# A two-layer token model on one core: mix and preparation in one block, the experts' first layer one group ahead, the last batch's routed rows scaled by VectorE

## The chip, the cores and the metric

One NeuronCore of one Trainium2 chip runs the whole program in one launch. The metric is device time in microseconds (us), lower is better. Engine names: TensorE (PE), its weight loads (PEld), VectorE (DVE), ScalarE (ACT), GpSimd (POOL), SyncE (SP). A line such as L1267 is a line of the kernel before.

## The reference, cut to what matters

The input is token numbers, 8 batches of 512; the model width D is 192. Six stages follow, each adding to a running stream `h`:

```python
h = tok_ref(x, ...)                                  # gathered rows, a trace of outer products
h = h + attn_ref(layernorm(h), ...)                  # linear attention
h = h + ffn_ref(layernorm(h), ...)                   # soft mixture of 64 experts
h = h + attn_q_ref(layernorm(h), ...)                # attention, 8-bit fake quantisation
x = h' + attention(layer_norm(h'), ...)              # h' = layernorm(h)
h = h + x + moe(layer_norm(x), top 2 of 8 experts)   # routed experts
```

In the soft mixture each of 64 experts gets one slot per batch: `h1 = gelu(xs @ w1 + b1)` (192 to 768), `ys = h1 @ w2 + b2` (768 to 192), and the rows are mixed back by `y = combine @ ys`. The quantised attention starts with `fake_quant(x) @ fake_quant(w_qkv)`: the scale of `x` is the largest absolute value of the normalised rows over all batches, divided by 127, and each weight matrix has such a scale of its own. In the last stage every row goes to the two experts with the largest logits.

## The kernel before, in words

`kernel_program` runs six stage functions one after the other. Each consists of blocks (`nc.Block`): in a block each engine has its own list of instructions with semaphores between them, and all engines meet at its end. After a stage, `recycle` adds a small block in which GpSimd clears semaphores.

**The experts' block of `soft_moe`** (L1205 to L1290). The 64 experts are taken in 16 groups of four (`GE` = 4, `NGR` = 16). The weights of one group are in one of three slots (`RING` = 3); a slot is filled in two parts by `ring_load` (L934): part 0 is the first layer with its bias (per expert 576 KB), part 1 the second layer (576 KB per expert), and both parts of a slot count on one semaphore. Groups 0 to 2 are sent in the block before. In this block SyncE sends part 0 of group g once the first layer of group g-3 is done, then part 1 once the second layer of g-3 is done (L1273 to L1277). TensorE's order for each group is:

- the first layer (L1245, L1248, L1253), after waiting for both parts of the slot (L1242)
- after ScalarE's gelu (L1228), six transposes (L1259)
- after VectorE's copy out of PSUM (L1217), the second layer in 48 small matmuls (L1267)

ScalarE then copies the result (L1232) and GpSimd stores it in DRAM (L1286). After the last group GpSimd loads everything back (L1289), and the block ends.

**The mix block** (L1295 to L1331). VectorE adds the second bias (L1299). For each batch TensorE multiplies four times (L1329), VectorE adds the product to the stream `m.H` (L1304) and takes statistics (L1308, four `bn_stats`), and ScalarE stages the next combine weights (L1317). The matmul buffers alternate between two batches.

**The preparation block of `quantised_attention`** (L1372 to L1431). VectorE turns all the statistics into means and variances in six linked steps (`ln_constants`, L151 to L156); ScalarE takes the square root (L430), VectorE the reciprocal (L425). Then VectorE normalises each batch (L1406, four instructions) and takes its absolute maximum (L1409), and takes the maxima of the two weight matrices (L1416, L1417); GpSimd reduces over the partitions (L1399); VectorE makes scales (L1369 to L1421), scales the weights (L1422, L1426) and rounds them to bf16 (L1423, L1425, L1427). GpSimd fills buffers with zeros and constants at the start of the block (L1391 to L1397). ScalarE begins the next block with L1447.

**The routed attention's last block** (L2369 to L2707). After the loop over batches, VectorE finishes the last batch: norm (L2564), stream sum (L2569), the two best experts (L2577 to L2585), the places of its rows (L2591 to L2602). GpSimd multiplies the normalised rows by the layer norm's gain and adds its offset (L2672, L2675), sends them by indirect transfers to DRAM, once for each of the two experts (`send`, L2687), and copies the last batch's rows (L2703) for the second of them. SyncE sends the weights of tiles 0 and 1 once the tile tables are made, waits for all sent rows, loads the rows of tiles 0 and 1 (`load_rows`, L2717, L2718), and sends the weights of tiles 2 and 3 (`load_weights`, L2724), and then the block ends.

**The routed experts' block** (L2743 on): 39 tiles of 256 rows. TensorE turns rows (L2781), computes first layers (L2791, L2795) one tile ahead and second layers (L2806). SyncE's loop is `next_rows(n)`, which waits until the rows of tile n-2 are copied, and from tile 4 on also `load_weights(n)`.

## Time and profile before

| | |
|---|---|
| time, median of 3 runs | 2439.43 us (2437.96 to 2439.54) |
| the profiled execution | 2437.44 us, of which the span is 2435.4 us |
| busy in it | PE 1882.9 us, DVE 1502.0, ACT 1057.0, POOL 398.8 |
| mean granted TensorE clock | 0.832 of full speed |
| experts' block (first layer to the last second layer) | 598.5 to 774.6 us |
| mix block, from VectorE's first work | 783.6 to 809.1 us |
| preparation block, to ScalarE's first work in the next | 809.1 to 839.7 us |
| last batch of the routed attention to the first routed tile | 2008.2 to 2057.6 us |
| routed tiles | 2057.6 to 2400.4 us |

How to read it: all times are from the span's start. The busy share of the page is a mean over stages with different limits, so each of the stretches is read by itself. A granted clock of 1.00 is 2.4 GHz and 0.50 is 1.2 GHz. In the timeline a line gives start, duration, engine, line and operation, and in brackets how long the engine was idle and what ended that. A row of busy time by stretch gives the stretch and its length, the busy time of PE, PEld, DVE, ACT and POOL (x instructions), the granted clock, the mean busy share of the 16 DMA engines (it can come out a little over 1) and GB/s.

### The profile page before, as it was taken

What the parts mean: (1) busy time and instruction counts of PE and PEld (TensorE: products, weight loads), DVE (VectorE), ACT (ScalarE), POOL (GpSimd) and SP (SyncE); (2) the same over time, 40 slices, a digit from 0 to 9 for tenths busy, and PEclk for the clock granted to TensorE, in tenths of its full rate; (3) what the DMA queues carried; (4) which work ended last, traced back from release to release, by engine and by line L of the source; (5) the groups of instructions that cost most, each with busy time, mean ns of one, the idle gap of its engine ahead of it and who ended that gap; (6) DMA issues with size and microseconds to landing.
All of it is one profiled execution on the core that took longest, in us unless ns stands there. A gap on an engine that the chain in (4) does not pass through costs nothing. (4 is left out here: it accounts for less than half of the span.)

```text
span 2435.4 us, 31261 instructions
## 1 busy us (share of the span) xinstructions
PE 1882.9 (77%) x9780; PEld 1010.5 (41%) x9804; DVE 1502.0 (62%) x2512; ACT 1057.0 (43%) x1856; POOL 398.8 (16%) x597
## 2 busy tenths in 40 slices
PE   3868789858886353777678857999899983999994
PEld 2735655535333320000112225443133333888883
DVE  4558459955101687999878874999788893111114
ACT  1100322213101267999889954333476660222221
POOL 5000000000221010222100003331023343222221
PEclk8989999969886575555589968997699995999997
DMA  3011110024994003333001007767777613566664
GB/s 84 1 38 33 52 33 18 20 90 165 403 410 194 13 1 125 126 125 125 26 19 39 26 15 113 121 118 118 85 86 98 99 30 129 177 203 204 203 206 182
DMA packets 147791, 264.96 MB, mean 109 GB/s; under 512 B 28865, under 2 KB 115986, under 8 KB 142679
## 3 DMA queue, kind: packets, MB, share of 16 engines
q1 hardware_dynamic: 135750, 242.10, 37.4%
q0 software_dynamic: 10768, 18.19, 2.3%
q10 hardware_dynamic: 1152, 3.15, 0.3%
q8 instruction: 67, 1.10, 0.2%
q14 instruction: 54, 0.43, 0.1%
HBM read 221.85 MB, written 57.71 MB: 115 GB/s over the span
## 5 line engine op out<-in xcount | busy, mean ns | idle before, releaser
L1677 PE MATMUL ps<-arena 128*128 x376 | 194.8, 621 | 108.0 <-ACT ps L1719 60.2
L1719 ACT ACTIVATE ps<-ps,arena 128x512 f32<-128x512 f32 x384 | 256.6, 1121 | 6.3 <-POOL arena L1703 6.3
L1687 DVE TENSOR_REDUCE arena<-ps 128x1024 f32 x192 | 232.8, 1224 | 24.1 <-PE ps L1677 9.9
L1719 ACT ACTIVATION_READ_ACCUMULATOR ps<-ps,arena 128x1 f32 x384 | 234.7, 668 | 0.0
L2151 DVE TENSOR_REDUCE arena<-ps 128x1024 f32 x192 | 221.0, 1216 | 10.7 <-PE ps L2314 8.4
L2520 ACT ACTIVATE arena<-ps 128x1024 f32<-128x1024 f32 x192 | 185.0, 1020 | 97.4 <-PE ps L2402 95.8
L2850 DVE TENSOR_TENSOR arena<-ps,arena 128x384 f32<-128x384 f32 x39 | 21.7, 557 | 286.9 <-PE ps L2806 286.9
L2830 ACT ACTIVATE arena<-ps,arena 128x256 f32<-128x256 f32 x234 | 89.5, 481 | 235.9 <-PE ps L2795 230.0
L2314 PE MATMUL ps<-arena 96*128 96x512 bf16 x500 | 163.8, 433 | 23.9 <-DVE arena L2151 11.1
L1884 ACT ACTIVATE arena<-ps 128x1024 f32<-128x1024 f32 x192 | 178.7, 1048 | 8.0 <-DVE arena L1904 4.6
L528 PE MATMUL ps<-arena 96*128 96x456 f32 (+1 forms) x512 | 169.9, 482 | 8.8 <-DMA arena<-la_xt 5.2
L2806 PE MATMUL ps<-arena 128*128 128x192 f32 x936 | 162.5, 330 | 0.7 <-DVE arena L2850 0.7
L2806 PEld LDWEIGHTS ps<-arena 128*128 128x128 f32 x936 | 151.0, 190 | 13.6 <-issue 13.6
L1904 DVE TENSOR_SCALAR arena<-arena 128x1024 bf16<-128x1024 f32 x192 | 128.5, 690 | 29.1 <-ACT arena L1884 14.9
L1677 PEld LDWEIGHTS ps<-arena 128*128 128x128 bf16 x384 | 25.6, 110 | 276.4 <-ACT ps L1719 197.5
L1837 PE MATMUL ps<-arena 128*128 (+1 forms) x368 | 113.6, 389 | 15.8 <-DMA arena<-arena 13.5
L528 PEld LDWEIGHTS ps<-arena 96*128 96x128 f32 x512 | 96.0, 196 | 71.4 <-issue 55.0
L2765 POOL DMA_INDIRECT routed_out<-arena x78 | 74.7, 958 | 283.2 <-DVE arena L2850 271.3
L1217 DVE COPY arena<-ps 128x768 f32<-128x768 f32 x16 | 15.3, 957 | 155.3 <-PE ps L1259 155.3
L2791 PE MATMUL ps<-arena 128*128 128x256 f32 x468 | 109.8, 385 | 0.9 <-DVE arena L2844 0.9
L2468 PE MATMUL ps<-arena 128*32 128x512 f32 x768 | 106.3, 626 | 4.0 <-ACT arena L2520 2.2
L2402 PE MATMUL ps<-arena 99*128 99x512 bf16 x384 | 104.8, 397 | 2.4 <-ACTq L137 2.4
(384 smaller groups left out, 3258.2 us busy)
## 6 DMA issues: line engine op xcount, KB each, us to landing
arena<-in_sm_w_dram SPq DMA_DIRECT2D x128, 576.0 KB
arena<-in_re_w_dram SPq DMA_DIRECT2D x39, 1252.0 KB, 5.8
arena<-ra_parts SPq DMA_DIRECT2D x192, 192.0 KB, 9.1
routed_in<-routed_in SPq DMA_DIRECT2D x8, 3332.0 KB, 14.2
ra_parts<-arena SPq DMA_DIRECT2D x48, 192.0 KB, 2.5
arena<-routed_in SPq DMA_DIRECT2D x39, 196.0 KB, 5.4
arena<-la_xt SPq DMA_DIRECT2D x16, 384.0 KB, 3.4
arena<-arena SPq DMA_DIRECT2D x64, 96.0 KB, 2.2
```

What stands on the lines that cost most here:

```text
L528: ins = pe.matmul(ps[:, 2 * (t % 2) + bank, to:to + w], XTs[j][:, c, t * P:(t + 1) * P], Wx[:, kind, c, at:at + w], start=(c == 0), stop=( ...
L1677: ins = pe.matmul(ps[:, 2 * (n % 4) + t % 2, :], QM[j][:, h, t * P:(t + 1) * P], KI[:, b, h // HG, :], start=True, stop=True)
L1687: v.tensor_reduce(MXq[:, b, 2 * u:2 * u + 2, at_head(h)], ps[:, 2 * (n % 4):2 * (n % 4) + 2, :], AX.X, ALU.max).then_inc(s_lk, 1)
L1719: ins = act.activation(bank, bank, ACT.Exp, bias=nb[n % 4][:, t % 2:t % 2 + 1], scale=c_reg, accum_out=RS[:, b, t, at_head(h):at_head(h) + 1])
L1837: ins = pe.matmul(ps[:, 2 * (n % 3) + q, :], QM[j][:, h, c * P:(c + 1) * P], QI[:, bass.ds(b, 1), g, :].rearrange("p o s -> p (o s)"), sta ...
L1884: act.activation(PF[n % 3], ps[:, 2 * (n % 3):2 * (n % 3) + 2, :].rearrange("p a s -> p (a s)"), ACT.Exp, scale=c_reg).then_inc(pe_.sem, 1)
L1904: v.tensor_scalar(PB[n % 3], PF[n % 3], MAGIC, MAGIC, ALU.add, ALU.subtract).then_inc(rd.sem, 1)
L2151: v.tensor_reduce(MX[:, bass.ds(b, 1), 2 * (n % 2):2 * (n % 2) + 2, n // 2].rearrange("p o t -> p (o t)"), ps[:, 2 * (n % 2):2 * (n % 2) + ...
L2314: ins = pe.matmul(ps[:, t, :], ST_[j][0][0:KR, h, t * P:(t + 1) * P], ST_[j][1][0:KR, h, :], start=True, stop=True)
L2520: act.activation(PF[e // 2 % 2][:, 2 * (e % 2):2 * (e % 2) + 2, :], ps[:, 2 * (e % 3):2 * (e % 3) + 2, :], ACT.Exp, scale=HD ** -0.5).then ...
L2791: pe.matmul(unit(k), wr[:, k * P:(k + 1) * P], XT[j][:, 0, :], start=True, stop=False)
L2806: ins = pe.matmul(ps[:, 7, h * D:(h + 1) * D], HT[j][:, k, h * P:(h + 1) * P], wr[:, at:at + D], start=(k == 0), stop=(k == KH - 1))
```

## The change

It has four parts.

1. In the experts' block part 0 of a slot gets a semaphore of its own. TensorE does the first layer of group g+1 before the transposes and the second layer of group g; only the second layer waits for part 1. VectorE and ScalarE follow that order, and SyncE sends part 0 of group g+1 ahead of part 1 of group g.
2. The mix block is removed, and its work is in the preparation block. The bias sum and the staged combine weights go to new buffers. Batches go in four pairs: mix, statistics, and the constants of that pair; ScalarE normalises (a scale and a bias for each row); VectorE takes the maxima of the pair before. The weights' maxima, scales and rounding stand between the pairs, and their scaling is ScalarE's. GpSimd reduces twice, first for the weights, then for the rows.
3. For the last batch VectorE multiplies and adds gain and offset, right after the stream sum, and ScalarE makes the copy.
4. The weights of tiles 2 and 3 are sent at the start of the routed experts' block.

The diff's core:

```diff
+    done = (m.ring_first, m.ring)[part][r]
     for q in range(GE):
-        sp.dma_start(m.EW[:, GE * r + q, w], io.sm_w[GE * g + q][:, w]).then_inc(m.ring[r], 16)
+        sp.dma_start(m.EW[:, GE * r + q, w], io.sm_w[GE * g + q][:, w]).then_inc(done, 16)
...
+            hidden(0)
+            for g in range(NGR):
+                if g + 1 < NGR:
+                    hidden(g + 1)
+                out(g)
...
             for g in range(RING, NGR):
-                hp.wait(sp, g - RING, 1)
-                ring_load(sp, m, io, B1, g, 0)
+                if g == RING:
+                    hp.wait(sp, g - RING, 1)
+                    ring_load(sp, m, io, B1, g, 0)
+                if g + 1 < NGR:
+                    hp.wait(sp, g + 1 - RING, 1)
+                    ring_load(sp, m, io, B1, g + 1, 0)
                 yp.wait(sp, g - RING, 1)
                 ring_load(sp, m, io, B1, g, 1)
...
+        @block.vector
+            v.tensor_tensor(YE, YB, b2[:, None, :].to_broadcast([NE, B, D]), ALU.add).then_inc(s_b, 1)
...
+            between = None, weight_maxima, weight_scales, round_weights
+            for k in range(NP):
+                mix(2 * k)
+                l(mix(2 * k + 1))
+                ln_constants(v, l, m.ST[:, two, :, :]..., mean, flat(m.var[:, two, :]))
+                v.sem_inc(s_var, 1)
+                if k:
+                    for b in (2 * k - 2, 2 * k - 1):
+                        row_max(b)
+                    between[k]()
+                v.wait_ge(s_std, k + 1)
+                l(v.reciprocal(rstd, work))
+                v.scalar_tensor_tensor(out=flat(m.wk[2][:, two, :]), in0=mean, scalar=-1.0, in1=rstd, ...
+            for b in (B - 2, B - 1):
+                row_max(b)
...
+        @block.scalar
+            for b in range(B):
+                act.activation(CS[:, b, :], CT[:, b, :], ACT.Copy).then_inc(cst.sem, 1)
...
+            for k in range(NP):
+                act.activation(m.wk[1][:, two, :], m.var[:, two, :], ACT.Sqrt, ...)
+                act.wait_ge(s_k, k + 1)
+                for b in (2 * k, 2 * k + 1):
+                    for t in range(T):
+                        ins = act.activation(m.X[:, b, t, :], m.H[:, b, t, :], ACT.Identity,
+                                             bias=m.wk[2][:, b, t:t + 1], scale=m.rstd[:, b, t:t + 1])
+                if k == 2:
+                    act.activation(Wf, Wf, ACT.Identity, bias=magic[0:DC], scale=inv[0:DC, 1:2])
+                    act.activation(WPf, WPf, ACT.Identity, bias=magic, scale=inv[:, 2:3])
...
-            load_weights(sp, io, m, 2)
-            load_weights(sp, io, m, 3)
...
+            def scale_last():
+                gt.wait(v, p, 2)
+                v.tensor_tensor(rows, rows, lg_[:, None, :].to_broadcast([P, T, D]), ALU.mult).then_inc(s_gb, 1)
+                v.wait_ge(s_gb, 2 * p + 1)
+                v.tensor_tensor(rows, rows, lb_[:, None, :].to_broadcast([P, T, D]), ALU.add).then_inc(s_gb, 1)
...
-                scale(p + 1)
+                if p + 1 < B - 1:
+                    scale(p + 1)
...
-            pool.tensor_copy(XA[B % 2][:, :, HEAD:RW], XA[1 - B % 2][:, :, HEAD:RW]).then_inc(s_gb, 1)
+            act.activation(XA[B % 2][:, :, HEAD:RW], XA[1 - B % 2][:, :, HEAD:RW], ACT.Copy).then_inc(s_gb, 1)
...
             for n in range(2, NW):
+                load_weights(sp, io, m, n)
+            for n in range(2, NW):
                 next_rows(n)
```

## Rows read from the trace of the kernel before

**Rows 1.** Busy time by stretch: the experts' block, and its loads' time.

```profile
598.50:774.60 176.10, 140.90 (x1440) 63.26 (x1440) 16.83 (x31) 19.04 (x32) 30.93 (x60) 0.84 0.89 353
605.50:757.50 152.00, 122.02 (x1266) 55.91 (x1265) 14.82 (x28) 15.96 (x28) 28.89 (x56) 0.85 1.02 405
```

**Rows 2.** Timeline of TensorE over the last two groups.

```profile
758.60 2.16 PE L1267 MATMUL ps<-arena 128*32 128x192 f32 x48 [1.05 <-DVE arena L1217]
761.81 0.88 PE L1245 MATMUL ps<-arena 4*128 4x384 f32 x2 [1.05 <-issue]
...
767.92 1.57 PE L1259 MATMUL ps<-arena 128*128 128x128 f32 x6 [0.97 <-ACT arena L1228]
...
770.54 4.07 PE L1267 MATMUL ps<-arena 128*32 128x192 f32 x48 [1.05 <-DVE arena L1217]
```

**Rows 3.** Busy time by stretch: two stretches in which the clock is low.

```profile
598.50:604.50 6.00, 5.66 (x36) 1.17 (x36) 0.00 (x0) 1.23 (x2) 0.00 (x0) 0.72 0.01 3
727.00:741.00 14.00, 11.98 (x90) 4.78 (x90) 1.06 (x2) 1.12 (x2) 0.63 (x2) 0.51 1.02 411
```

**Rows 4.** Timeline of the mix block, VectorE.

```profile
783.62 1.75 DVE L1299 TENSOR_TENSOR arena<-arena 64x1536 f32<-64x1536 f32 x1 [13.13 <-PEq L1205]
...
788.89 0.96 DVE L1304 TENSOR_TENSOR arena<-ps,arena 128x768 f32 x1 [3.52 <-PE ps L1329]
...
791.47 0.96 DVE L1304 TENSOR_TENSOR arena<-ps,arena 128x768 f32 x1 [0.30 <-PE ps L1329]
```

**Rows 5.** Groups by line: normalising, maxima, and a small ScalarE copy.

```profile
L1406 DVE TENSOR_SCALAR arena<-arena x32 | 10.0, 374 | 0.5 <-DVE arena L425 0.5
L1409 DVE TENSOR_REDUCE arena<-arena x8 | 7.6, 952 | 1.3 <-DVE arena L1406 1.3
...
L1232 ACT ACTIVATE arena<-ps 128x192 f32<-128x192 f32 x16 | 5.3, 330 | 87.9 <-PE ps L1267 87.9
```

**Rows 6.** Timeline of the preparation block.

```profile
811.22 0.88 DVE L156 TENSOR_SCALAR arena<-arena 128x32 f32<-128x32 f32 x1
...
812.18 1.28 ACT L430 ACT_TABLE_LOAD   x1 [9.88 <-DVE arena L156]
...
833.19 1.34 DVE L1416 TENSOR_REDUCE arena<-arena 96x1 f32<-96x1152 f32 x1
...
838.51 0.46 DVE L1427 TENSOR_SCALAR arena<-arena 128x576 bf16<-128x576 f32 x1
839.73 1.03 ACT L1447 ACTIVATE arena<-arena 128x768 f32<-128x768 f32 x1 [25.93 <-DVEq L137]
```

**Rows 7.** Timeline of the routed attention's last batch.

```profile
2018.38 0.17 DVE L2557 TENSOR_SCALAR arena<-arena 128x4 f32<-128x4 f32 x1
...
2021.84 1.89 POOL L2687 DMA_INDIRECT routed_in<-arena  x1 [0.64 <-POOL arena L2680]
...
2028.43 0.19 DVE L2571 TENSOR_SCALAR arena<-ps 128x32 f32<-128x32 f32 x1 [5.61 <-PE ps L2429]
...
2029.44 1.80 POOL L2675 TENSOR_TENSOR arena<-arena 128x768 f32<-128x768 f32 x1
2029.74 1.52 DVE L2582 CAST arena<-arena 128x8 f32<-128x8 uint32 x1
...
2031.56 0.69 DVE L2585 TENSOR_TENSOR arena<-arena 128x32 bf16<-128x32 f32 x1
...
2034.71 1.03 POOL L2687 DMA_INDIRECT routed_in<-arena  x1 [2.42 <-DVE arena L2602]
```

**Rows 8.** Timeline from the last rows' load to the routed tiles.

```profile
2053.13 0.57 SPq L2718 DMA_DIRECT2D arena<-routed_in  x1
2054.46 1.48 SPq L2724 DMA_DIRECT2D arena<-in_re_w_dram  x2
2057.60 1.09 PE L2781 MATMUL ps<-arena 128*128 128x128 f32 x4 [24.93 <-DVEq L137]
...
2066.93 0.66 PE L2781 MATMUL ps<-arena 128*128 128x128 f32 x4
```

More of the change, by code:

```diff
@@ L1223, in _, with gelu @@
             yc.start(act)
-            for g in range(NGR):
+            def gelu(g):
                 j = g % 2
@@ L1290, in _ @@
             pool.wait_ge(s_ty, 16)
[L1292 to L1331 removed]
+    m.mix = CT, YB, b2
 def quantised_attention(nc, m, io):
@@ L1401, in _, with mix @@
         @block.vector
         def _(v):
-            ln_v(v)
-            with v.Fori(0, B) as b:
+            hh.start(v)
+            l = Link(v, s_ch)
+            flat = lambda a: a.rearrange("p b t -> p (b t)")
+            v.tensor_tensor(YE, YB, b2[:, None, :].to_broadcast([NE, B, D]), ALU.add).then_inc(s_b, 1)
+            def mix(b):
+                yo.wait(v, b, 1)
+                v.tensor_tensor(m.H[:, b, :, :], ps[:, b % 2 * T:b % 2 * T + T, 0:D], m.H[:, b, :, :],
+                                ALU.add).then_inc(hh.sem, 1)
+                hh.wait(v, b, 1)
@@ new lines, in _ @@
+            for k in range(NP):
+                mix(2 * k)
+                l(mix(2 * k + 1))
+                two = slice(2 * k, 2 * k + 2)
+                mean, rstd, work = (flat(a[:, two, :]) for a in (m.mean, m.rstd, m.wk[1]))
+                ln_constants(v, l, m.ST[:, two, :, :].rearrange("p b t s -> p (b t) s"), work, flat(m.wk[0][:, two, :]),
+                             mean, flat(m.var[:, two, :]))
+                v.sem_inc(s_var, 1)
[5 more added lines that the diff above has]
+                l(v.reciprocal(rstd, work))
+                v.scalar_tensor_tensor(out=flat(m.wk[2][:, two, :]), in0=mean, scalar=-1.0, in1=rstd, op0=ALU.mult,
+                                       op1=ALU.mult).then_inc(s_k, 1)
```

152 lines of the change are left out of this document (83 added, 69 removed).

## The prediction, as it stands on record

> **What bounds the kernel now.** I read the page first, for the stages, then busy time by stretch, then the timeline at the ends of the stretches that the change touches. The page's chain of waits covers only the last 30 us, so each place is read by itself.
>
> In the experts' block the transfers are the bound, though TensorE looks busy. From 605.5 to 757.5 us the DMA share is 1.02 at 405 GB/s, while PE is busy 122.0 of 152.0 us [rows 1]. The loads of 13 groups (52 experts, twice 576 KB each, 61.3 MB) at 405 GB/s take 151.5 us, which is the stretch: 11.6 us a group. TensorE needs less: 140.9 us busy for 16 groups is 8.8, and 9.9 with the wait for VectorE's copy (1.05) that stays. But see the end. TensorE sits idle for 1.05 us and starts the last group's first layer at 761.81, put down to nothing that the trace shows; gelu, slots and buffers were ready long before, so I take it for the last load, landed by about 761.7. Then the whole group follows, and the last second layer starts at 770.54 and ends at 774.61 [rows 2].
>
> The mix is bound by TensorE, 2.58 us a batch with VectorE waiting 0.30 in each [rows 4]. The preparation is one chain on VectorE: statistics, a table load, eight normalised batches, eight maxima, the weights [rows 5, 6]. In the routed attention's last batch the chain goes over VectorE's places to GpSimd's eight sends, then SyncE, then a block's end [rows 7, 8].
>
> **The experts' block.** With the new order the last first layer, its gelu and its transposes wait only for part 0, sent two parts before the last one, so nothing but the second layer is left when the last part lands. Does it land sooner? Bytes are the same and the DMA engines are full; SyncE's wait for part 1 now stands behind a wait for the next first layer, but that one comes earlier in TensorE's list, and some five parts stay queued. So no change: 761.7. If TensorE runs group 14's second layer late, the turn (1.57) and VectorE's copy follow it [rows 2], so I take the last second layer's start at 761.5 from one and 762.7 from the other, nearest the landing. That is 770.54 - 761.6 = 8.9 us, rounded to **9.0**. Ends: 4.9, if TensorE gets slower (first rival), and 11, if the last layer takes 2.16 as the one before it instead of 4.07.
>
> **Mix and preparation.** Before: from 783.62 to ScalarE's first work at 839.73, 56.1 us [rows 4, 6]. After, from the same start:
> - first stream sum at 5.3 (783.62 to 788.89), the second at 7.9, paced by TensorE; then TensorE is ahead and a batch costs VectorE 2.58 - 0.30 = 2.28 [rows 4]. First pair done at 10.1.
> - Constants of a pair: six links at 0.17 [rows 7] and some 0.03 between them, 1.2. The table load 1.28 comes once [rows 6], the root and hand-offs about 0.45, reciprocal and product 0.4: 13.5.
> - Three more pairs: 2 x 2.28 + 1.2 + two maxima at 0.95 [rows 5] + 0.4 = 8.1 each, 24.3: 37.8. The roots are ready by then, behind the maxima.
> - Between them: weights' maxima 1.34 and, for half the columns, 0.7 [rows 6]; scales 0.45; rounding, 0.46 for 576 columns [rows 6], 1728 columns, 1.4. Sum 3.9: 41.7.
> - The tail: ScalarE normalises batches 6 and 7, eight times 0.33 [rows 5], 2.7, then the last maximum 0.95, and 0.4 of links: 45.8. GpSimd's reduction as before 0.6, three links 0.6, the block's end 0.76 (838.97 to 839.73 [rows 6]): 47.7.
> - The semaphore clearing now stands ahead of this block: 0.4 more, 48.1.
>
> Gain **8.0**. What leaves VectorE is 32 normalisings at 0.374 [rows 5] and two weight scalings; what comes is three more sets of constants. ScalarE's weight scaling (1728 columns at 1.03 for 768 [rows 6], 2.3 us) stands behind batch 5, under VectorE's fourth pair. SyncE's and GpSimd's fills are over before the weights' maxima, at 21 us. There is no row of ScalarE normalising out of the stream; if one costs 0.5, the tail grows by 1.4. Ends: 4.6, with that and a start 2 us later, and 9.
>
> One cost at the start: GpSimd fills its buffers beside VectorE's bias sum. In the trace VectorE's step at 811.22 took 0.88 instead of 0.17 beside a fill [rows 6, 7], and the one at 2029.74 lasted until GpSimd's sum ended [rows 7], but both have one input; the two-input steps beside the same fill ran on. I take 0, with 2 us as the end. The Trainium skill (GPSIMD Engine Reference, Key points) says that GpSimd's SBUF interfaces are shared with VectorE, with contention for instructions with two SBUF inputs too. By that the bias sum would start late and the gain be about 6.
>
> **The last batch.** VectorE's two scalings fall into its idle 5.61 us ahead of the logits [rows 7]: two of about 0.96, free. They slow the four sends of the batch before, as one was slowed to 1.89 [rows 7], by up to 1.9 us; these still end about 1 us before the places. GpSimd's sum and copy are gone, so the cast of 1.52 becomes 0.17 and the sum of 0.69 becomes 0.19: places, sends (from 2034.71), weights and landing all come **1.8** earlier. ScalarE's copy is ready before the second four sends. Ends: 0, if the slowed sends come last, and 2.3.
>
> **The two weights.** SyncE's last work before the block's end is now the rows' load, over at 2053.70 instead of 2055.94: **2.2** us off the way to TensorE's start at 2057.60 [rows 8]. Moved behind it: SyncE sends 1.48 us plus register reads before the rows of tile 2, which go about 3 us after the block's start; they land within 5.5, and their turn is 9.3 after the start (2066.93) [rows 8]. Hidden, by 1 us. Ends: 0.7, if they are late, and 2.3. From there TensorE is the bound through 39 tiles, and all of it shifts.
>
> **Sum.** 9.0 + 8.0 + 1.8 + 2.2 = 21.0. The profiled execution took 2437.44, of which 2435.4 are span; 2437.44 - 21.0 = 2416.4. The median lies 2.0 above that execution: 2418.4.
>
> **The rivals.**
> 1. *TensorE becomes the bound of the experts' block.* Its room is small: 598.5 + 16 groups must end by 765.6 (761.5 + 4.07), so 10.4 us a group against 9.9 now. If it spends more time at 1.2 GHz, which it did from 727 to 741, with 12.0 of 14.0 us busy and the clock at 0.51 [rows 3], and a group averages 10.7, it ends at 769.7: 4.9 instead of 9.0, time 2422.5. For it: it will wait for parts in the last groups. Against it: a TensorE that falls behind doesn't wait, and then has the pattern of now. Chance 0.13.
> 2. *Half clock from the first group on, and the sum turns.* A group is then first layer 5.66 [rows 3], turn 1.57, wait 1.05, second layer 4.07 [rows 2]: 12.35, over the 11.6 of the transfers. 598.5 + 16 x 12.35 = 796.1 against 774.6: 21.5 slower there, 12.0 faster elsewhere, time 2448.9. It decides the sign where a group averages over 11.8 (176.1 + 12.0 by 16). For it: half clock came right inside busy stretches. Against it: the mean clock was 0.84 [rows 1] with a longer wait in each group than stays. The Trainium skill (TensorE: Matmul & The Clock Gate, HAM oscillation) describes this loss for loops that wait for each weight slice; by it every group would start cold. Chance 0.04.
> 3. *The merged block gains nothing*: hand-offs between VectorE and ScalarE, four times over, take back the 8. Time 2426.4. Against it: each pair has two maxima between variance and root. Chance 0.06.
> 4. *The experts' block gains nothing*, because the last part lands later or the stores queue: 2427.4. Chance 0.05.
> 5. *It doesn't do what it says*: no gain beyond what can be told. Chance 0.03.
>
> **The numbers.** A measurement can tell 0.2%, 4.9 us, from no change. The forecast, all four gains with 14 to 25 us, has 0.69. Faster: 0.69 + 0.13 + 0.06 + 0.05 = 0.93; same 0.03; slower 0.04. The low ends sum to 10.2, the high ends to 24.6, and not all fall together. The range is 2414 to 2427: 25 to 12 us; it takes in rivals 1 and 3.
>
> **What would show it.** Right: the last second layer starts within 1.5 us of the last load; from VectorE's bias sum to ScalarE's first work 46 to 50 us, with one table load; VectorE's cast at 0.17; TensorE's first turn some 3.9 us sooner after the last batch's start. Wrong: a clock well under 0.84 in the experts' block, VectorE idle for ScalarE in pairs two to four, the first sends of the last batch waiting for GpSimd itself, or a gap before the turn of tile 2.

## The result, and the profile after

The changed kernel takes 2413.71 us (median of 4 runs, 2409.40 to 2419.60) against 2438.69 us (4 runs, 2435.74 to 2439.54) in the same rounds: a ratio of 0.9893, 95% interval 0.9872 to 0.9913, so 25.0 us faster. It was measured twice more, with 6 runs each: 0.9899 [0.9877, 0.9921] and 0.9906 [0.9876, 0.9937]. The direction held, the forecast of 2418.4 is 4.7 us too high, and the median lies 0.3 us below the range (2414 to 2427). That is far less than these runs can tell: the first interval alone is a gain of 21 to 31 us. The profiled execution took 2415.31 us, 22.1 less than the one of before.

| step of the program | before | after | difference | predicted |
|---|---|---|---|---|
| experts' block, first matmul to the end of the last second layer | 176.0 | 164.9 | -11.1 | -9.0 |
| from there to VectorE's bias sum | 9.0 | 9.4 | +0.4 | +0.4 |
| bias sum to ScalarE's first work in the next block | 56.1 | 45.8 | -10.3 | -8.4 |
| last batch: MAX8 of the batch before to the first of its sends | 26.5 | 24.7 | -1.8 | -1.8 |
| that send to the first load of rows | 16.0 | 16.1 | +0.1 | 0 |
| that load to TensorE's first turn | 6.9 | 4.9 | -2.0 | -2.2 |

The parts sum to 24.7. The rest of the 22.1 is code that the change doesn't touch: the experts' block began 1.6 us later, and the stages up to the last batch and the end took 0.8 and 0.3 more.

**Experts' block.** Busy time by stretch, inside the block and over it; columns as in [rows 1].

```profile
607.10:757.00 149.90, 120.61 (x1300) 52.71 (x1292) 14.82 (x28) 16.77 (x29) 28.89 (x56) 0.86 1.02 408
600.10:765.10 165.00, 132.87 (x1440) 58.42 (x1440) 16.74 (x30) 19.02 (x32) 30.94 (x60) 0.87 0.94 376
```

The DMA engines are as full as before (1.02, 408 GB/s against 405 in [rows 1]). TensorE's timeline at the block's end answers to [rows 2]:

```profile
751.92 0.91 PE L1259 MATMUL ps<-arena 4*128 4x384 f32 x2
...
758.09 2.16 PE L1285 MATMUL ps<-arena 128*32 128x192 f32 x48 [1.05 <-DVE arena L1225]
760.18 1.07 PE L1276 MATMUL ps<-arena 128*128 128x128 f32 x6
762.91 2.16 PE L1285 MATMUL ps<-arena 128*32 128x192 f32 x48 [1.66 <-DVE arena L1225]
```

The last first layer (751.92) is now two second layers ahead. TensorE idles 1.66 us before the last second layer where 1.05 is usual. VectorE's copy for it was over at 762.25, and the part is the only other thing that it still waits for, so I put the 0.6 us down to the last part (the trace doesn't name it). Nothing is left behind that part but this layer. It takes 2.16 us, where the last one of before took 4.07. In the groups of TensorE over the whole block the wait for ScalarE's gelu (15.6 us before) is gone. In its place stand 14.6 us that the trace puts down to nothing ("issue"), ahead of first layers, which I take for waits for parts; the run with one semaphore below names the loads at such places.

```profile
L1259 PE MATMUL ps<-arena 4*128 4x384 f32 x64 | 35.0, 632 | 16.2 <-issue 14.6 <-DVE arena L1215 1.6
L1285 PE MATMUL ps<-arena 128*32 128x192 f32 x768 | 34.5, 328 | 17.4 <-DVE arena L1225 17.4
```

Four of these waits are 3.3 to 3.6 us long, and behind each of them the matmuls run at 1.2 GHz (two took 0.88 us at the block's start and take 1.61 here). The last of the four:

```profile
739.76 1.61 PE L1259 MATMUL ps<-arena 4*128 4x384 f32 x2 [3.33 <-issue]
```

**Mix and preparation.** VectorE's timeline, cut to the links of the sum (answers to [rows 4, 6]):

```profile
774.48 1.75 DVE L1415 TENSOR_TENSOR arena<-arena 64x1536 f32<-64x1536 f32 x1 [12.23 <-PEq L115]
779.24 0.96 DVE L1419 TENSOR_TENSOR arena<-ps,arena 128x768 f32<-128x768 f32 x1 [3.02 <-PE ps L1406]
...
786.96 0.20 DVE L1464 RECIPROCAL arena<-arena 128x8 f32<-128x8 f32 x1 [1.79 <-ACT arena L1484]
787.20 0.17 DVE L1465 SCALAR_TENSOR_TENSOR arena<-arena 128x8 f32<-128x8 f32 x1
787.28 0.95 DVE L1419 TENSOR_TENSOR arena<-ps,arena 128x768 f32<-128x768 f32 x1
788.26 1.14 DVE L1423 BATCH_NORM_STATS2 arena<-arena 128x6 f32<-128x192 f32 x4
789.32 0.94 DVE L1419 TENSOR_TENSOR arena<-ps,arena 128x768 f32<-128x768 f32 x1
...
815.54 0.95 DVE L1428 TENSOR_REDUCE arena<-arena 128x1 f32<-128x768 f32 x1 [1.93 <-ACT arena L1489]
```

From 787.28 on VectorE hardly waits; two sums follow each other at 2.04 us. ScalarE's rows beside it:

```profile
785.33 1.28 ACT L1484 ACT_TABLE_LOAD   x1 [6.70 <-DVEq L1458]
787.40 3.62 ACT L1489 ACTIVATE arena<-arena 128x192 f32<-128x192 f32 x8 [0.47 <-DVE arena L1465]
820.29 1.03 ACT L1511 ACTIVATE arena<-arena 128x768 f32<-128x768 f32 x1 [3.03 <-DVEq L137]
```

**Last batch and first tiles.** The timeline of GpSimd, VectorE and TensorE (answers to [rows 7, 8]):

```profile
2003.21 1.88 POOL L2762 DMA_INDIRECT routed_in<-arena  x1 [0.64 <-POOL arena L2755]
2005.40 1.75 POOL L2762 DMA_INDIRECT routed_in<-arena  x1 [0.30 <-issue]
2007.45 0.96 POOL L2762 DMA_INDIRECT routed_in<-arena  x1 [0.30 <-issue]
2014.24 0.98 POOL L2762 DMA_INDIRECT routed_in<-arena  x1 [2.98 <-DVE arena L2677]
```

```profile
2005.35 0.96 DVE L2637 TENSOR_TENSOR arena<-arena 128x768 f32<-128x768 f32 x1 [1.17 <-PE ps L2483]
2006.35 0.96 DVE L2639 TENSOR_TENSOR arena<-arena 128x768 f32<-128x768 f32 x1
2011.11 0.18 DVE L2657 CAST arena<-arena 128x8 f32<-128x8 uint32 x1
```

```profile
2035.28 1.09 PE L2857 MATMUL ps<-arena 128*128 128x128 f32 x4 [23.08 <-DVEq L137]
2045.42 0.66 PE L2857 MATMUL ps<-arena 128*128 128x128 f32 x4 [0.74 <-DMA arena<-routed_in]
2046.20 2.83 PE L2867 MATMUL ps<-arena 128*128 128x256 f32 x12
```

Two sends of the batch before are slow. The one of 1.88 us lies beside VectorE's stream sum (2003.23, 0.96 us) and was as slow before (1.89); only the one of 1.75, beside the two scalings, is new. The other two keep 0.96 and the last of the four ends at 2009.68, well ahead of 2014.24. The cast falls from 1.52 to 0.18. The turn of tile 2 waits 0.74 us for its rows, which the prediction took to have landed by then.

### The profile page after: what moved, and what is told of

Its sections match the earlier page's. It is cut to its first block and busy times, and to the rows that moved or that the text cites. A ratio compares the mean times of both kernels' runs of the same rounds, so it can differ in the third digit from the quotient of the medians.

```text
span 2413.4 us, 31067 instructions
## 1 busy us (share of the span) xinstructions
PE 1875.3 (78%) x9780; PEld 1005.5 (42%) x9804; DVE 1495.3 (62%) x2507; ACT 1074.2 (45%) x1894; POOL 394.8 (16%) x595
## 5 line engine op out<-in xcount | busy, mean ns | idle before, releaser
L2882 PEld LDWEIGHTS ps<-arena 128*128 128x128 f32 x936 | 151.0, 190 | 13.6 <-issue 13.6
```

Source lines behind the costliest of these rows:

```text
L2882: ins = pe.matmul(ps[:, 7, h * D:(h + 1) * D], HT[j][:, k, h * P:(h + 1) * P], wr[:, at:at + D], start=(k == 0), stop=(k == KH - 1))
```

## The experiments

Blocks are measured in each profiled execution; "block" is the experts' block from its first matmul to the end of its last second layer.

**The changed kernel again.** No edit.

> The changed kernel once more, timed in five rounds, to see how far its single times lie apart. In the two profiled executions at hand (2437.4 and 2415.3 us) the four parts account for 22 us: 11.1 in the experts' block, 10.3 in mix and preparation, 1.8 and 2.0 at the last batch and the two weights, less some 3 us of drift in code that is the same. Theory 1 (the gain is 22 to 23 and the 25.0 of the medians is the spread of few runs): ratio 0.990 to 0.992. Theory 2 (something outside the four parts gained 2 to 3 us more, which the profiled execution happened to miss): ratio 0.987 to 0.989. Theory 3 (the spread from 2409 to 2420 is TensorE's clock): the mean granted clock of the single runs orders their times.

Median 2413.24 (6 runs, 2405.36 to 2423.08), ratio 0.9899. The ratio, with an interval of 0.9877 to 0.9921, doesn't decide between the first two theories. The times of the six follow the mean clock but for one pair, as the third has it. The profiled execution has a block of 170.7 us, not 164.9. Its merged block is 45.8 again.

**One part at a time.** Each is the kernel before with the hunks of part 1; part 2; parts 3 and 4.

> The kernel before with part 1 alone (first layer a group ahead, a semaphore for each part of a slot). From the block's first matmul to the end of the last second layer 176.0 us before and 164.9 in the changed kernel. Theory 1 (the end is the last load plus one second layer): 163.5 to 167, with the last second layer starting 155 to 156 us after SyncE's first load in the block; time 9 to 12 us less. Rival (TensorE became the bound after the change, its clock decides): the last second layer starts at once behind the one before it, with no wait, and the stretch varies with the clock, 167 to 175; time 3 to 8 less.

> The kernel before with part 2 alone (mix and preparation in one block). From VectorE's bias sum to ScalarE's first work in the next block 56.1 us before and 45.8 in the changed kernel. Theory 1 (this part is worth what this stretch shows): the stretch 45.5 to 46.5, time 9 to 11 us less. Rival (part of the 10.3 came from a different state that part 1 leaves behind, such as the clock or the stores): stretch 48 to 50, time 6 to 8 less, as the prediction had it.

> The kernel before with parts 3 and 4 alone (last batch's rows scaled by VectorE, two weights sent later). Theory 1: 1.8 us sooner at the first of the last batch's sends and 2.0 us less from the first rows' load to TensorE's first turning, together 3.8 us less at the end of the tiles, and no wait for the rows of tile 2 beyond what the gelu's table load covers; time 3.5 to 4 less. Rival (the later weights delay the rows of tile 2 and the gain of part 4 is given back there): 1.8 to 2.5 less.

| kernel | median | ratio, interval | what its profile shows |
|---|---|---|---|
| part 1 | 2429.34 | 0.9966 [0.9949, 0.9983] | block 165.3 |
| part 2 | 2430.15 | 0.9969 [0.9949, 0.9989] | bias sum to next block 45.8, block 176.2 |
| parts 3, 4 | 2432.96 | 0.9983 [0.9967, 0.9999] | rows' load to the first turn 5.3, block 174.0 |

The ratios give 8.3, 7.6 and 4.1 us, each with 4 to 5 us to both sides, 20.0 together against 24.6 for the whole in the same rounds: the parts add up within what these intervals can tell, and each of them gains, the last only just clear of nothing. The stretches came out where the first theories put them, but for the rows' load to the first turn (1.7 us less instead of 2.0). Executions of one kernel spread over 9 to 20 us, so a term of 1 to 2 us can only be read in a stretch of a profile, not in a median. Much of the spread goes with TensorE's mean clock: the four runs of after are 2409.4, 2412.1, 2415.3 and 2419.6 at 0.839, 0.837, 0.836 and 0.833.

**The first layer waits for both parts** (is it the separate semaphore that gains, or TensorE's new order?).

```diff
                 pe.wait_ge(m.ring_first[g % RING], FIRST_LOAD * (g // RING + 1))
+                pe.wait_ge(m.ring[g % RING], RING_LOAD * (g // RING + 1))
```

> The changed kernel, but TensorE waits for both parts of a slot ahead of the first layer, as before; the order of the layers stays. The question is which half of part 1 pays. Theory 1 (the gain lies in what is left to do after the last load): the last first layer now starts only when part 1 of the last group has landed, some 162.5 us after the block's first matmul, and behind it come that layer (4.2 to 5.7), the transposes, copy and second layer of group 14 and those of group 15 (4.3 to 6.7 each): the block takes 175 to 181 us, at least as long as before (176.0), and the whole gain of part 1 is gone, 9 to 14 us more than the changed kernel. Rival (the gain lies in TensorE's bubbles that the new order fills): the block takes 165 to 170 us and the time is within 3 us of the changed kernel.

2428.40 (9 runs), ratio 0.9954 [0.9935, 0.9974]; block 182.0. The waits of TensorE in the block:

```profile
PE ps L1260 <- DMA arena<-in_sm_w_dram: 18.3, 10, 3.0
PE ps L1286 <- DVE arena L1225: 16.8, 16, 1.1
```

By the ratio 11.2 us are left of the whole change, and parts 2, 3 and 4 alone gave 11.7, so the whole gain of part 1 is gone. The block can't be set beside the 176.0 of the kernel before, since this execution began at 1.2 GHz (see below); beside the changed kernel's 170.7, which began so too, it is 11.3 us longer. With the new order alone a first layer waits for the part that is sent last, and two groups' work stands behind it: the last such wait ends at 763.16, the block at 785.19.

**SyncE's order of before** (part 0 of group g, then part 1 of g) under TensorE's new order.

```diff
-                if g == RING:
-                    hp.wait(sp, g - RING, 1)
-                    ring_load(sp, m, io, B1, g, 0)
-                if g + 1 < NGR:
-                    hp.wait(sp, g + 1 - RING, 1)
-                    ring_load(sp, m, io, B1, g + 1, 0)
+                hp.wait(sp, g - RING, 1)
+                ring_load(sp, m, io, B1, g, 0)
```

> The changed kernel, but SyncE sends part 0 and part 1 of each group in the order of before. The last part 0 then lands one part, 5.8 us, before the end of the transfers instead of two. Theory 1 (behind the last part 0 TensorE has a chain of 12.7 us at full clock, 18.6 at half: first layer, transposes, copy and second layer of groups 14 and 15): the block ends 7 to 13 us after the last load: 169 to 175 us, 4 to 6 more than with the new order at the same clock. Rival (only the last part counts, since TensorE has caught up by then): 164 to 167.

2426.66 (10 runs), ratio 0.9945 [0.9926, 0.9963], so by the ratios 1.7 us of part 1's 8.3 are left; block 180.0, longer than the 169 to 175 that I expected. SyncE's timeline shows one half of why:

```profile
603.41 1.99 SPq L941 DMA_DIRECT2D arena<-in_sm_w_dram  x4
605.45 0.40 SPq L943 DMA_DIRECT2D arena<-in_sm_b_dram  x1
617.20 4.09 SPq L941 DMA_DIRECT2D arena<-in_sm_w_dram  x8
```

```profile
610.00:620.00 10.00, 8.95 (x90) 4.24 (x74) 1.06 (x2) 1.14 (x2) 2.16 (x4) 0.66 0.25 81
```

Part 0 of group 4 could go after two first layers, but stands behind part 1 of group 3, which needs a second layer. So 13.8 us lie between the first and the next loads (part of it the clock, 0.66 in that stretch), and the DMA engines are busy 0.25 of the ten shown. Summed from the GB/s of the trace in steps of 1 us, 61 of the block's 62.1 MB had moved 163.7 us after its start, against 156.1 in after: 7.6 us later. The other 7.5 of the 15.1 us lie behind that, and they are what was expected: the last first layer waits for its part until 762.23, and the work of two groups follows it, much of it at 1.2 GHz.

**The square root's table early.** ScalarE takes the root of one column ahead of its first wait for the pairs.

```diff
+            act.activation(spare_root, m.eps, ACT.Sqrt)
             act.wait_ge(s_b, 1)
```

> The changed kernel with one more ScalarE instruction: a square root of one column right after the staged combine weights, so that the table is loaded before the first pair's variances are there. Theory 1 (in the first pair VectorE stands for 1.79 us, of which 1.28 is the table load): VectorE's idle time before the first reciprocal falls to 0.4 to 0.6 and the stretch from its bias sum to ScalarE's first work in the next block from 45.8 to 44.4 to 44.6. Rival (something else is late by as much, TensorE's third batch or ScalarE itself): the stretch stays above 45.3.

2413.76 (4 runs), ratio 0.9901 [0.9868, 0.9935]: not to be told from the changed kernel by the median, but the stretch is 44.5 instead of 45.8, and VectorE's wait before the first reciprocal falls from 1.79 to 0.51:

```profile
784.14 0.20 DVE L1465 RECIPROCAL arena<-arena 128x8 f32<-128x8 f32 x1 [0.51 <-ACT arena L1486]
```

**The six transposes of group g ahead of the first layer of g+1** (hides VectorE's copy, 1.05 us a group).

```diff
             for g in range(NGR):
+                turn(g)
                 if g + 1 < NGR:
                     hidden(g + 1)
                 out(g)
```

> The changed kernel with TensorE's transposes of group g ahead of the first layer of group g+1 instead of behind it. VectorE's copy (0.96 and 1.05 of waiting) then lies beside the first layer, and behind the last part 0 two pieces less are left: first layer, second layer 14, transposes, copy, second layer 15, 10.6 us at full clock and 16.4 at half, against 11.6 for the two last parts. Theory 1 (in the executions where the changed kernel's block takes 165 us it waits for the last load, where it takes 171 TensorE's chain behind the last part 0 is what ends last): the block takes 164 to 167 us, TensorE's waits for VectorE's copy are under 3 us in all 16 groups instead of 17, and the time is 1 to 4 us under the changed kernel. Rival (the clock alone sets it, since longer waits for parts make it fall): a mean clock in the block under 0.83 and no gain.

2413.13 (6 runs), ratio 0.9892 [0.9869, 0.9914]. TensorE's wait of 1.05 is gone in nearly all groups, yet the block is 170.6 us; the last second layer now waits for its part alone (the copy for it was over at 768.23):

```profile
769.61 2.16 PE L1288 MATMUL ps<-arena 128*32 128x192 f32 x48 [2.38 <-issue]
```

So that part landed at about 769.5, 168.3 us after the block's start, where in after it landed at about 162.7. Bytes and rate are the same, and the transfers started later. SyncE's first loads in the changed kernel, in the two profiled executions, first the one with 164.9 us:

```profile
605.97 1.95 SPq L941 DMA_DIRECT2D arena<-in_sm_w_dram  x4
...
610.00 1.77 SPq L941 DMA_DIRECT2D arena<-in_sm_w_dram  x4
...
614.17 5.88 SPq L941 DMA_DIRECT2D arena<-in_sm_w_dram  x8
```

and the one with 170.7 us (block from 603.54):

```profile
611.17 1.95 SPq L941 DMA_DIRECT2D arena<-in_sm_w_dram  x4
...
618.66 1.95 SPq L941 DMA_DIRECT2D arena<-in_sm_w_dram  x4
...
623.20 6.11 SPq L941 DMA_DIRECT2D arena<-in_sm_w_dram  x8
```

Their stretches, same order (first the changed kernel, then its repeat):

```profile
610.00:620.00 10.00, 8.11 (x96) 4.13 (x96) 1.86 (x3) 1.95 (x3) 2.27 (x4) 1.00 1.02 399
```

```profile
600.00:610.00 10.00, 8.41 (x45) 2.93 (x51) 0.68 (x3) 1.87 (x2) 0.00 (x0) 0.50 0.01 2
610.00:620.00 10.00, 9.93 (x58) 2.79 (x42) 0.03 (x1) 1.62 (x2) 0.00 (x0) 0.52 0.68 244
```

In the repeat TensorE is at 1.2 GHz (0.50, 0.52) when the block begins, so the first buffers come free later and the DMA engines are busy only 0.68 of the second ten us. But the repeat ends otherwise than turns first and after:

```profile
757.66 0.88 PE L1259 MATMUL ps<-arena 4*128 4x384 f32 x2 [3.14 <-issue]
...
766.03 4.01 PE L1285 MATMUL ps<-arena 128*32 128x192 f32 x48 [1.05 <-DVE arena L1225]
769.97 1.07 PE L1276 MATMUL ps<-arena 128*128 128x128 f32 x6
772.09 2.16 PE L1285 MATMUL ps<-arena 128*32 128x192 f32 x48 [1.05 <-DVE arena L1225]
```

Its last second layer waits for VectorE's copy alone. What ends last is TensorE's own work behind the last first-layer part, partly at 1.2 GHz: 16.6 us from 757.66 to the end, where after needs 13.2. That is what the first theory of this run expected of executions of 171 us. The transfers have their share too: 61 MB have moved after 159.7 us in the repeat, 156.1 in after, 161.8 in this run. So of the 5.8 us between the two lengths some 3.6 are later transfers and some 2.2 are work behind them. The next theory was about the start of the transfers alone.

**The first layer of one group twice**, group 0 in one kernel, group 8 in the other.

```diff
+                for again in range(2 if g == 0 else 1):
...
```

> The changed kernel, with the first layer of the experts' group 0 computed twice in a row (the second time starts its sums anew, so the values are the same): 18 more TensorE instructions right at the start of the experts' block, 4.2 us at full clock and 5.7 at half. Nothing else differs. Theory 1 (the length of the experts' block is set by when the ring's first buffers come free: in the profiled executions of three kernels with this SyncE order, part 1 of group 3 went 14.0, 19.7 and 20.8 us after the block's first matmul, and the block ended 164.9, 170.7 and 170.6 after it, each time 150 to 151 later): every ring load shifts by the repeat, the DMA engines can't make it good since they are full from there on, and the block ends 150 to 152 us after part 1 of group 3 goes, so 169 to 171 us long where the first groups run at full clock, 175 to 177 where they run at half. Theory 2 (TensorE's waits for parts in the last groups swallow it, since TensorE needs about 9.9 us a group against 11.6): the block stays at 164 to 166 at full clock, the end less than 150 after that load.

> The changed kernel, with the first layer of the experts' group 8 computed twice instead of once: the same 4 to 6 us of TensorE work as in the run before, but in the middle of the block, where the DMA engines are full and some five parts are queued ahead. Theory 1 (only work of TensorE ahead of the first ring loads lengthens the block): the end stays 150 to 152 us after part 1 of group 3 goes; 165 us long at full clock in the first groups, 171 at half. Theory 2 (TensorE's own work bounds the block, and any addition lengthens it): 4 to 6 us longer than that, and the DMA share falls below 1.0 for some microseconds behind group 8.

One run each, 2414.39 and 2417.66 us. What they show stands in the last table of this section.

**Part 0 expert by expert at the start.** In groups 0 and 1 TensorE takes the first layer expert by expert and signals each; SyncE follows. With the early table.

```diff
+                for q in range(GE - 1):
+                    sp.wait_ge(s_ex, (GE - 1) * (r - RING) + q + 1)
+                    sp.dma_start(m.EW[:, GE * (r % RING) + q, 0:HID + HH],
```

> The changed kernel with two additions. (a) In groups 0 and 1 TensorE computes the first layer expert by expert and signals after each, and SyncE sends part 0 of groups 3 and 4 expert by expert behind these signals; before, it waited for the whole group's first layer, and the DMA engines stood idle for the block's first 7 us. (b) ScalarE computes one square root of one column ahead of the merged block's work, which brings its table early (measured before: 1.2 us off that block). Theory 1 (the block's length is set by the start of the ring loads): the first of them goes some 2 us after the block's first matmul instead of 5.8, the DMA share is 1.0 from about 4 us on instead of 7, and the block ends 3 to 3.5 us sooner: 161.5 to 162.5 at full clock in the first groups. With (b) 4 to 4.7 us less in all: median about 2409, if the clock falls as in the other runs, and a ratio about 0.2% below that of the changed kernel. Theory 2 (something else ends the block: the landing of the last part depends on the last buffers' release, not on the first): the block stays at 164 to 166 us, and only (b)'s 1.2 us are seen.

2424.07 (6 runs), ratio 0.9926 [0.9904, 0.9948]: by the ratios 5 to 8 us slower than the changed kernel, where 4 us faster was expected. TensorE's timeline, first this kernel, then after:

```profile
615.06 1.48 PE L1264 MATMUL ps<-arena 128*32 128x384 f32 x4
616.47 0.84 PE L1268 MATMUL ps<-arena 64*32 64x384 f32 x4
```

```profile
606.62 0.85 PE L1262 MATMUL ps<-arena 128*32 128x384 f32 x8
609.03 0.88 PE L1267 MATMUL ps<-arena 64*32 64x384 f32 x16
```

By expert, four matmuls take 1.48 us; in the order of after eight take 0.85, both at a granted 1.00 (the trace has each of these matmuls twice, so four are the two of one expert and eight are one of each expert). The first group's layer took 12.9 us, the first 5 us of it at 1.2 GHz, against 5.6 or 7.5 in the order of after, and part 1 of group 3 went 27.4 us after the start instead of 14.0.

**Part 0 in three steps behind TensorE's unchanged order.** One signal after each half of the 128-row part, with the early table.

```diff
+                    if g < 2:
+                        ins.then_inc(s_ex, 1)
...
+                        for half in range(2):
+                            sp.wait_ge(s_ex, 2 * (r - RING) + half + 1)
+                            for q in range(GE):
+                                w = slice(half * HH, (half + 1) * HH)
```

> The changed kernel, its square root table brought early, and in groups 0 and 1 a signal after each half of the first layer's 128-row part, in the order of TensorE's work as it is (it is not taken expert by expert: that took 12.9 us instead of 5.6 to 7.5 for a group, since two products in a row for one expert don't overlap). SyncE sends part 0 of groups 3 and 4 in three steps behind these signals: columns 0 to 383, 384 to 767, the rest. Theory 1 (the block's length is set by the start of the ring loads and the gap between the first two): where the first groups run at full clock, the first step goes 1.7 us after the block's first matmul instead of 5.8, the DMA engines are busy without a gap from about 3 us on instead of 7, and the block is 161 to 162.5 us long; at half clock the first step goes at 3.2 us, part 1 of group 3 still at 19.7, and the block is 168 to 169.5 instead of 171. The profiled stretch shows which. The merged block 44.6 instead of 45.8. In all 3 to 5 us less than the changed kernel of the same call, so a ratio about 0.0015 below its ratio. Theory 2 (the last buffers' release sets the end, not the first loads): block 165 or 171, and only 1.2 us less.

> The changed kernel as it is, on the same chip and in the same rounds as the run before, to compare the two and to see again which of two lengths the experts' block has. Theory 1 (the clock of TensorE in the block's first groups decides): the block is 165 us long where the first layer of group 0 takes 5.6 us, and 171 us where it takes 7.4, and part 1 of group 3 goes 14.0 or 19.7 us after the block's first matmul, with the end 150 to 152 us behind it. Median 2413, within 2410 to 2416.

Both ran on another chip, on which the kernel before takes 2420.89 (11 runs). Thirds: 2395.63 (6 runs), ratio 0.9896 [0.9864, 0.9927]. Changed: 2398.85 (6 runs), 0.9906 [0.9876, 0.9937]. Its median lay outside the 2410 to 2416 that I gave, with that of the kernel before; the ratio is the old one.

**Rows of tiles 2 and 3 ahead of their weights.**

```diff
             for n in range(2, NW):
-                load_weights(sp, io, m, n)
-            for n in range(2, NW):
                 next_rows(n)
+                load_weights(sp, io, m, n)
```

> The changed kernel, with SyncE sending the rows of routed tiles 2 and 3 ahead of their two weights instead of behind them. Tests whether the wait of 0.74 us ahead of the turn of tile 2 costs the change anything. Theory 1 (it is hidden: the next first layer waits for gelu and its table load anyway): no wait for the rows ahead of that turn, but the next first layer starts as long after the first tile's turn as in the changed kernel (10.9 us), within 0.2. Theory 2 (it is on the path): 0.5 to 0.7 us sooner. Everything else is that of the changed kernel, so its time is within that kernel's spread, 2405 to 2423.

2420.64 us, one run. The turn of tile 2 no longer waits, and the next first layer starts as before or later:

```profile
2050.11 0.66 PE L2856 MATMUL ps<-arena 128*128 128x128 f32 x4
2051.68 2.83 PE L2866 MATMUL ps<-arena 128*128 128x256 f32 x12 [0.92 <-DVE arena L2919]
```

That is 11.1 us after the first turn (2040.55) against 10.9 in after (2035.28 to 2046.20). So the wait of 0.74 us is not on the path, as far as one profile of each can tell.

**The block's length against its first loads**, from the profiled execution of each kernel, in us after the block's first matmul:

| kernel | clock in the first group | first load | part 1 of group 3 | 61 MB moved | block | block less part 1 of group 3 |
|---|---|---|---|---|---|---|
| after | 2.4, then 1.2 GHz | 5.8 | 14.0 | 156.1 | 164.9 | 150.9 |
| part 1 alone | same | 5.8 | 14.0 | 156.1 | 165.3 | 151.4 |
| root early | same | 5.8 | 14.0 | 156.2 | 164.7 | 150.7 |
| changed, third time | same | 5.8 | 14.0 | 156.2 | 166.3 | 152.3 |
| changed, again | 1.2 GHz | 7.6 | 19.7 | 159.7 | 170.7 | 151.0 |
| group 8 twice | 1.2 GHz | 7.6 | 19.7 | 159.9 | 170.2 | 150.6 |
| rows first | 1.2 GHz | 7.6 | 19.6 | 159.4 | 171.0 | 151.4 |
| turns first | 1.2 GHz | 7.6 | 20.8 | 161.8 | 170.6 | 149.8 |
| group 0 twice | 2.4, then 1.2 GHz | 9.8 | 18.0 | 160.2 | 170.6 | 152.6 |
| by expert | 1.2, then 2.4 GHz | 6.5 | 27.4 | 166.7 | 177.0 | 149.6 |
| by thirds | 1.2 GHz | 3.1 | 19.7 | 159.1 | 167.5 | 147.8 |

The last column is 149.8 to 152.6 us wherever part 0 is sent whole: repeating the first layer of group 0 costs 5.7 us (170.6 against 164.9), repeating that of group 8 nothing (170.2 against 170.6 to 171.0 at the same clock). So work of TensorE ahead of the first loads lengthens the block, and the same work in its middle doesn't.

That it is the start of the transfers alone isn't shown. In the executions of 170 to 171 us, turns first apart, the 61 MB are through 3.3 to 4.1 us later than in after, and the block is 5.3 to 6.1 us longer. And the last second layer waits longer than the usual 1.05 us only in after, root early, changed (third time) and turns first; in the others TensorE's own work ends last.

The thirds, meant as the test from the other side, don't settle it. Their block is 2.7 to 3.5 us shorter than the four of that clock (it was expected at 168 to 169.5), and their first load goes 4.5 us sooner. But the small pieces move more slowly (328 GB/s at a share of 0.99 from 10 to 15 us, where the repeat has 418 at 1.01), and the 61 MB are through only 0.3 to 0.8 us sooner than in three of the four. Most of the 3 us lies behind the transfers, in TensorE's work at the end, with a granted 0.89 in the last 15 us against 0.66 to 0.77 in these three.

## Why the prediction was right, and where it was wrong

**What failed, in the whole.** The direction held, and so did the mechanisms in the profiled pair, but for what hides the rows of tile 2. The steps that failed are the sizes of two terms, both put too small: the last second layer, kept at 4.07 us (it took 2.16), and the price of an unwaited batch in the mix, put at 2.28 us (it took 2.04, six times). The four steps gained 24.7 us instead of 21.0, which is 3.7 of the 4.7 us that the forecast was too high, and these two terms are 3.3 of the 3.7. Of the rest, code that the change doesn't touch took back 2.6 in the profiled execution, and 3.6 are chance: the median lies 1.6 us below the profiled execution, where I had put it 2.0 above. So the miss of the range by 0.3 us says little by itself; the two terms are read from the stretches.

**Experts' block, 9.0 forecast; 11.1 in the first profile, 5 in others, 8.3 [4, 12] by the ratio of part 1 alone.** The mechanism held in the profiled pair: the last first layer is off the end, and nothing but a second layer stands behind the last part. The start of that layer was forecast 163.0 us after the block's start (761.6 less 598.61), and is at 162.7. The failing step is the size of the last layer: I kept the 4.07 us of [rows 2] and had 2.16 as the bound. That is 1.9 of the 2.1 us. Of the three profiles with the order of before, that layer took 4.07, 3.8 and 2.16, so the row that I stood on was no constant; which clock the last layer gets is luck as far as these runs show (it took 3.81 in the third profile of the changed kernel). What the prediction didn't have at all is the dependence on the clock at the start: it asked whether the last part lands sooner, and left out that it can land later. In the new order an execution that begins at 1.2 GHz has a block 5.8 us longer, some 3.6 by later transfers and some 2.2 by TensorE's work behind the last first-layer part, which then ends last. Seven of the thirteen profiled executions with TensorE's new order began so. Those with the order of before (three) all began at 2.4 GHz, so what it would cost there stays open, as does why the clock is low then: in the repeat it fell during the stage before (0.58 from 595 to 600 us), though TensorE had been as busy in the 5 us before as in after (3.84 in both).

**Mix and preparation, 8.0 forecast, 9.9 measured** (10.3 less the 0.4 of the clearing), 45.8 in all ten profiles of this block without the early root, against 47.7 forecast. The step that failed is "a batch costs VectorE 2.28": I took the wait of 0.30 off the period of 2.58, but the sum then also starts before the statistics' last instruction has wholly ended, and a batch costs 2.04. Six such batches are 1.4 us. The first pair came at 12.8 instead of 13.5 (first sum 4.8 after the start, not 5.3; second at 7.3, not 7.9), and against that ScalarE's normalising from SBUF takes 3.62 for eight, 0.45 each instead of 0.33, which VectorE waits for only in the tail (1.93 and 0.80 before the last two maxima; the tail took 6.7 us instead of 6.0). The table load was on the path with its whole 1.28 us, as the early root showed (45.8 to 44.5), and the prediction had it there. The bias sum took 1.75 us beside GpSimd's fills, as long as before, so the 2 us bound was not needed. The Trainium skill (GPSIMD Engine Reference, Key points), by which it would start late, doesn't show in this step; these fills only write (their rows have no source), so the step says nothing of GpSimd work that reads.

**Last batch, 1.8 forecast, 1.8 measured; two weights, 2.2 forecast, 2.0 measured.** Cast and sum came as costed, and only one more send was slowed. Only the cover of tile 2's rows was misjudged: they are 0.74 us late, but behind them stood a second cover that I hadn't named. ScalarE's first gelu, behind its table load, sets the next first layer: that layer starts 0.98 to 0.99 us after the gelu in all three profiles (2067.53 and 2068.51 before, 2045.21 and 2046.20 after, 2050.70 and 2051.68 with the rows first), and running the rows first removed the wait and gained nothing.

**The rivals.** In the first profile TensorE did not become the bound in the way of the first: it waits for parts (14.6 us in all). In the executions of 170 to 171 us, turns first apart, it is TensorE's work that ends last, behind a late part, so there a share of that rival came true. Half clock from the first group on was the second's condition, and it did come in many executions, but at a stretch only for the first two groups, with another price: 5.8 us, not 21. Its sum was also too low for its own condition: the 5.66 us of [rows 3] is a first layer at a mean 0.72, and at 1.2 GHz it took 7.46 (603.54 to 611.00 in the repeat). The Trainium skill (TensorE: Matmul & The Clock Gate, HAM oscillation) describes a loop in which every slice starts cold behind a wait for its transfer. After agrees in four groups, each cold behind a wait of 3.3 to 3.6 us; the groups that waited only the copy's 1.05 didn't start cold, and the whole stretch has a granted 0.86. In the repeat, matmuls behind such a wait began at 2.4 GHz and fell to 1.2 some 1.6 us later (757.66 and 759.25). The third and fourth fall with the single parts' ratios and with their stretches.

**The range.** Its low end was 25 us of gain. The profiled steps sum to 24.7 and the medians differ by 25.0. The two upper misses, 1.9 and 2.1 us, have the same sign, and I had let only 4 us of upward error in, since "not all fall together".

**The fastest version.** The one with the thirds and the early root is 3.2 us below the changed kernel by the medians of the same rounds; the ratios' intervals overlap by far, so no gain of the whole is shown. What is shown is the 1.3 us of the early root (44.5 instead of 45.8 in three profiles). For the thirds there is one profile, 167.5 from a start at 1.2 GHz; the changed kernel beside it had 166.3 from a start at 2.4.

## What to carry to other kernels

Where a stage is bound by transfers, cost three things: the start of the first transfer that has to wait for a buffer, the bytes at the full rate, and the work behind the last landings. The start and the end hang on the compute engine and its clock even where the middle doesn't. And look at each of the last landings, not only the last: here TensorE's work behind an earlier part outlasted the last landing in most executions. The new order of work, the separate semaphore and the order of sends belong together: the changed kernel without the semaphore, or with the old order of sends, was some 10 to 15 us slower by the ratios, which within the intervals is all that part 1 gains (8.3). The semaphore alone, with TensorE's order of before, was not run.

When a wait is taken off a steady loop, don't subtract it from the period. Look for a stretch of the trace in which the same instructions run without a wait, and if there is none, widen the bound on the side of the gain.

## What I had not expected of the hardware

- Recorded matmuls of 384 columns took 0.37 us a piece (1.48 for four) where one expert's stand together, all to the same 32 rows of PSUM, and 0.11 (0.85 for eight) where they go round the four experts and their four groups of rows, at the same granted clock. Why is not shown: the 16 of L1267 also go to the same 32 rows for each expert, from different halves of the input rows, and took 0.88 together. Reordering a nest for an early signal cost more than the signal brought.
- The same program shows two lengths of one block, 165 to 166 and 171 us, by which of its two levels TensorE's clock has when the block begins.
- Weight loads in pieces of 192 KB kept the DMA engines as busy as those of 576 KB (a share of 0.99 and 1.01) and moved 328 GB/s instead of 418.
- VectorE runs the next sum 0.1 us before the last of four statistics has ended (787.28, 788.26 + 1.14, 789.32): an unwaited batch costs 2.04, less than the sum of its instructions, 2.09.
- GpSimd's indirect sends took 1.75 and 1.88 us instead of 0.96 beside two-input work of VectorE on 768 elements, and that work kept its 0.96.
